# FFN sums of squares: from GpSimd arithmetic to ScalarE squares and accumulating DMAs, in a fused decoder layer

## The reference, cut to what matters

```python
# per batch entry; xf: 512 x 512, h: 512 x 2048
h    = silu(gate(xf)) * up(xf)
inv  = rsqrt(mean(h * h, axis=-1) + eps)          # RMS norm over the 2048 hidden features
y    = (h * inv) @ w_proj.T
x    = layernorm(x + y)
```

## Time and profile before

| | |
|---|---|
| median of 3 runs | 1694.94 us (1691.09 to 1696.45) |
| the profiled execution: its own time | 1689.61 us |
| its span in the trace | 1687.9 us |
| busy: PE, DVE, ACT, POOL | 1235.4, 1269.3, 710.4, 788.3 us |
| FFN squares (L493) and adds (L498) on POOL | 95.0 us in 60 squares (4 more write RD), 121.7 us in 60 adds |
| mean granted TensorE clock | 0.832 of full |

### The profile page before, as it was taken

One profiled execution on the slowest core, in us unless ns is written; L12 is line 12 of the kernel. 1 busy time (PEld: TensorE's weight loads), 2 busy tenths in 40 slices (PEclk: granted clock), 3 DMA queues, 4 the chain that ended last, 5 costly groups with the idle time before them and its releaser, 6 DMA issues.

```text
span 1687.9 us, 13988 instructions
## 1 busy us (share of the span) xinstructions
PE 1235.4 (73%) x4570; PEld 576.9 (34%) x4570; DVE 1269.3 (75%) x1296; ACT 710.4 (42%) x1038; POOL 788.3 (47%) x496
## 2 busy tenths in 40 slices
PE   5564656787887847789786866878797874778696
PEld 4332222333444412333443422323343421323353
DVE  5878879799658876779649885769838887789634
ACT  6773325353354432534363441535354432544221
POOL 1002654244359663334249764334239774334244
PEclk7766878788898977789799986779798886889798
DMA  6742795545136585455236477455235468355132
GB/s 207 261 161 81 163 226 113 129 100 125 53 91 152 114 199 141 101 118 110 67 96 134 111 181 196 88 112 113 69 100 127 112 163 216 89 113 125 36 97 81
DMA packets 108697, 213.88 MB, mean 127 GB/s; under 512 B 13664, under 2 KB 24416, under 8 KB 108624
## 3 DMA queue, kind: packets, MB, share of 16 engines
q1 hardware_dynamic: 89248, 144.95, 30.0%
q0 software_dynamic: 18432, 67.12, 20.8%
q10 hardware_dynamic: 944, 0.92, 0.2%
HBM read 116.08 MB, written 29.62 MB: 86 GB/s over the span
## 4 chain that ended last, share of the span: by engine, by line
DVE 32%; PE 31%; DMA 10%; issue 8%; POOL 6%; ACT 3%; SPq 1%; ACTq 0%; POOLq 0%; DVEq 0%
PE ps L1401 11%; DVE ST L835 11%; DVE MX L891 4%; PE ps L1371 4%; PE ps L1209 4%; DVE ST L838 4%; DMA YA<-ST 4%; DMA GU<-gu_tiles 4%; POOL ST L432 3%; PE ps L1226 3%; DVE QS L1021 2%; DMA KS<-qk_parts 2%; DVE BST L871 2%; PE ps L1315 1%; PE ps L1288 1%
## 5 line engine op out<-in xcount | busy, mean ns | idle before, releaser
L835 DVE TENSOR_TENSOR_SCAN ST<-dA,ST 128x1024 f32<-128x1024 f32 x128 | 383.9, 2999 | 66.8 <-POOL ST L432 49.3
L432 POOL TENSOR_TENSOR ST<-DU,BC 128x1024 f32<-128x1024 f32 x128 | 369.2, 2885 | 134.3 <-issue 61.5
L1401 PE MATMUL ps<-V,GU 128*128 128x512 f16 x1024 | 246.6, 397 | 20.9 <-DMA GU<-gu_tiles 15.2
L446 POOL DMA_DIRECT2D YA<-ST x128 | 112.4, 878 | 301.8 <-DVE ST L838 297.3
L1209 PE MATMUL ps<-KS,QS 96*128 96x512 f32 x256 | 136.1, 607 | 156.4 <-DVE MX L891 73.3
L891 DVE TENSOR_REDUCE MX<-ps 128x1 f32<-128x512 f32 x256 | 165.1, 686 | 111.2 <-PE ps L1209 111.1
L554 ACT ACTIVATE dA<-DL,Aneg 128x511 f32<-128x511 f32 x256 | 167.4, 713 | 142.2 <-DVE ST L835 142.1
L838 DVE TENSOR_TENSOR ST<-ST,BC 128x1024 f32<-128x1024 f32 x128 | 220.8, 1725 | 4.4
L1371 PE MATMUL ps<-WP,QS 128*128 128x512 f32 x512 | 156.1, 453 | 58.3 <-DVE QS L1021 55.2
L685 ACT ACTIVATE PT<-ps 128x1024 f32<-128x1024 f32 x128 | 125.2, 1020 | 138.7 <-PE ps L1315 138.0
L493 POOL TENSOR_TENSOR QAK<-QAK 128x512 f32<-128x512 f32 x60 | 95.0, 1584 | 138.2 <-DVE QAK L1030 138.2
(11 more groups left out here) (220 smaller groups left out, 1704.8 us busy)
## 6 DMA issues: line engine op xcount, KB each, us to landing
YA<-ST POOLq DMA_DIRECT2D x128, 512.0 KB, 5.2
BC<-bc_rows SPq DMA_DIRECT2D x64, 512.0 KB, 5.3
qk_parts<-PT SPq DMA_DIRECT2D x64, 256.0 KB, 5.2
GU<-gu_tiles SPq DMA_DIRECT2D x64, 256.0 KB, 3.6
WP<-proj_tiles SPq DMA_DIRECT2D x64, 256.0 KB, 2.7
QS<-qk_parts SPq DMA_DIRECT2D x48, 256.0 KB, 5.6
KS<-qk_parts SPq DMA_DIRECT2D x48, 256.0 KB, 7.5
ST<-in_L_ffn_w_gate_up_dram SPq DMA_DIRECT2D x16, 256.0 KB, 3.3
```

The costliest lines, as they stand in the source:

```text
L432: nc.gpsimd.tensor_tensor(ST[:, ring(bb, n, a), :, :], DU[:, 2 * a:2 * a + 2, :], BC[:, n % 2, 0:1, :].broadcast_to((P, 2, S)), ALU.mult). ...
L835: nc.vector.tensor_tensor_scan(flat, dA[:, a, :, :].rearrange("p e s -> p (e s)"), flat, 0.0, ALU.mult, ALU.add).then_inc(s_scan, 1)
L1401: last = mm(ps[:, f % F_RING, :], GU[:, t % 2, k, m * P:(m + 1) * P], XHL[:, z, k, :], start=(k == 0 and z == 0), stop=(k == KT - 1 and z ...
```

## The change

POOL's squares and adds go. ACT makes the square of tile t-1 right behind the silu of tile t (tile 15's behind the last HL copy). Square 0 is written into RD. Squares 1 to 15 alternate between two buffers, SQ (even tiles) and a part of PT (odd tiles). POOL adds squares 1 to 14 into RD by accumulating DMAs of 256 KB, each issued when its square is made (`s_sq`) and the accumulation before has landed (`s_acc`, now counted in 16s). ACT writes a buffer again when the DMA that read it has landed. Square 15 isn't accumulated: the final product with ones takes it as a second term, 8 matmuls where there were 4.

```diff
-        SQ = QAK[:, 4, :]
+        SQ = [QAK[:, 4, :], PT[:, 1, 0, :]]
...
+        def squares(t):
+            return RD[:, :] if t == 0 else SQ[t % 2]
+        def sums_landed(b, t):
+            return 16 * (NT - 2) * b + 16 * t
...
                     if not last:
                         for n, a in tile_halves(t):
                             half_step(b + 1, n, a)
-                    pool.wait_ge(s_h, NT * b + t + 1)
-                    if t > 0:
-                        pool.wait_ge(s_acc, NT * b + t)
-                    dst = RD[:, :] if t == 0 else SQ
-                    nc.gpsimd.tensor_tensor(dst, HT[:, t % 2, :], HT[:, t % 2, :], ALU.mult).then_inc(s_sq, 1)
-                    pool.wait_ge(s_sq, NT * b + t + 1)
-                    if t == 0:
-                        pool.sem_inc(s_acc, 1)
-                    else:
-                        nc.gpsimd.tensor_tensor(RD[:, :], RD[:, :], SQ, ALU.add).then_inc(s_acc, 1)
+                    if 0 < t < NT - 1:
+                        pool.wait_ge(s_sq, NT * b + t + 1)
+                        since(pool, s_acc, sums_landed(b, t - 1))
+                        nc.gpsimd.dma_start(RD[:, :], squares(t), accum_op=ALU.add).then_inc(s_acc, 16)
...
+                def square(t):
+                    if t > 2:
+                        act.wait_ge(s_acc, sums_landed(b, t - 2))
+                    nc.scalar.square(squares(t), HT[:, t % 2, :]).then_inc(s_sq, 1)
+
                 for t in range(NT + 1):
                     if t > 0:
                         act.wait_ge(s_h, NT * b + t)
                         if t > 2:
                             act.wait_ge(s_dn, NT * b + t - 2)
                         nc.scalar.copy(HL[:, (t - 1) % 2, :], HT[:, (t - 1) % 2, :]).then_inc(s_hh, 1)
+                        if t == NT:
+                            square(NT - 1)
                     if t < NT:
...
                         nc.scalar.activation(SG[:, t % 2, :], ps[:, (2 * t) % F_RING, :], ACT.Silu).then_inc(s_sg, 1)
+                        if t > 0:
+                            square(t - 1)
...
-                pe.wait_ge(s_acc, NT * (b + 1))
+                pe.wait_ge(s_sq, NT * (b + 1))
+                pe.wait_ge(s_acc, sums_landed(b + 1, 0))
...
                 for r in range(KT):
-                    last = mm(ps[:, 3, r:r + 1], RD[:, r * P:(r + 1) * P], ones[:, 0:1], start=True, stop=True)
+                    mm(ps[:, 3, r:r + 1], RD[:, r * P:(r + 1) * P], ones[:, 0:1], start=True, stop=False)
+                    last = mm(ps[:, 3, r:r + 1], squares(NT - 1)[:, r * P:(r + 1) * P], ones[:, 0:1], start=False, stop=True)
```

## The result

The changed kernel took 1718.06 us (median, 1713.79 to 1723.42) against 1693.01 (1689.70 to 1696.45) for the kernel before, run beside it: ratio 1.0127, 95% interval 1.0094 to 1.0159. The profiled execution took 1713.79 us, its span is 1712.0 at a mean granted clock of 0.830. The forecast was 1677, 1662 to 1697, so the sign was wrong. Of all runs in this document one, an execution of e11 at 1701.27 us, counts as slow (over 1.5% above the fastest of its kernel) and is left out of its ratio.

What follows compares the result with a forecast made beforehand. The prediction took POOL to bound tiles 8 to 16 of three FFN phases. Pairs -9.5, entry -3.0, exit -6.0 and last entry +0.9 gave -17.6 us: 1672 for the profiled execution, 1677 as a median, range 1662 to 1697.

Steps and rivals of the forecast that it cites:

- What bounded the kernel before: Tiles 8 to 16 of three FFN phases: POOL, busy 76.34 of 79 us, with slack in the DMA loop.
- The failed step: Tiles 9 to 15: the pair's tile without a load to wait for hides, so two tiles take 16.5 us.
- the exit: Tiles 15 and 16: the last scan's wait for `dBu` goes; gain of 2.0 us (0 to 3) per entry.
- The nine pairs: Three two-tile intervals, tiles 9 to 15, in each of three entries: 16.5 us for 17.6, -9.5 us in all.
- The road over GU: Tiles 9 to 15: loop product, GU load, gate product, silu, square, `dBu`, scan, product takes 15.95 us before load delay.
- rival 1: Tiles 9 to 15: GU load pays for the whole accumulation, +1.4 for +0.5 us, total 1685 us; chance 0.18.
- rival 2: Tiles 9 to 15: PE's clock falls ahead of the gate product, 1.4 us later; total 1694 to 1703; chance 0.22.
- The rule on the queues' turns: DMA engines alternate between queues packet by packet, so full POOL and SP queues share evenly; 0.5 us allowed for new traffic.
- The entry: Entry to the stage of tiles 8 to 16: first scan's wait and stretching go; gain 1.0 us (0 to 2.5) each.
- The last entry: Last FFN phase: tiles keep PE's pace of 5.33 us, with +0.95 us at the end for the doubled final product.
- rival 3: Last entry: accumulations don't keep PE's pace, about 1.0 us for each of 12 tiles, total 1689 us; chance 0.05.

Runs made afterwards that it cites:

- e11: Changed kernel, but POOL makes the squares instead of ACT, the accumulating transfers staying: 1686.88 us, ratio 0.9929 to the kernel before.
- e3: Changed kernel without the accumulations and their waits, so the squares of tiles 1 to 14 aren't summed: 1683.41 us, ratio 0.9919.
- e7: Kernel before the change, with the GU load issued ahead of the BC row: 1699.51 us, ratio 1.0011.
- e8: Changed kernel with ACT's square of tile t-1 ahead of the silu of tile t: 1709.65 us, ratio 1.0054.
- e15: Changed kernel with POOL's `dBu` held until DVE's product of the half step before is done: 1714.62 us, ratio 1.0102.
- e5: Changed kernel with the GU load issued ahead of the BC row: 1697.33 us, ratio 0.9993; once more 1698.82, 1.0011.
- e10: Changed kernel with square ahead of silu, GU load ahead of BC row, and `dBu` held behind DVE's product: 1652.90 us, ratio 0.9734.
- e2: Changed kernel with each accumulation moving only 32 of 512 columns, all waits and issues kept: 1701.27 us, ratio 1.0047.
- e4: Changed kernel with POOL adding ACT's squares by its own instruction in place of the accumulating DMA: 1703.55 us, ratio 1.0051.
- e6: Changed kernel with each accumulation issued a tile later and moving only 32 of 512 columns: 1703.41 us, ratio 1.0023.
- e9: Changed kernel with both square ahead of silu and GU load ahead of BC row: 1664.60 us, ratio 0.9816.

## Why the prediction was wrong

**What bounded the kernel before** held. POOL set its stage: with part of its work removed e3 and e11 are faster, and e7 shows that the GU road had slack. One reading was loose: POOL's operations run one behind the other, so it is DVE's that stretch them, not each other.

**The failed step** is this one: "The other tile of the pair hides: its gate product follows the down product without a load to wait for, so its square is done about when the scan before it ends." The fact in it was right (square done 540.86, scan end 541.48). The conclusion was not: a `dBu` released at that moment runs beside the product, and the product lasts 2.74 us longer, with the BC row and the GU load of the next odd tile waiting for its end. In the first pair of each entry the `dBu` started 0.5 to 1.0 us behind the product (525.38 behind 524.42 in entry 0) and didn't lengthen it; those are the pairs of 16.6 to 17.1. In the others the product of tile 13 took 3.97, 4.04 and 3.97, and the scan of tile 15 took 5.27, 4.92 and 5.28. The same in "the exit", where I allowed for up to 2.34 into the scan of tile 15 and it was 2.98. The nine pairs were to give -9.5 us (-1.05 each) and gave +19.9. e8 shows that a square that comes earlier only moves the meeting.

This meeting is not the whole price. Taken away alone (e15) it comes back as waits, and the pairs stay at 19.7. With the GU load ahead alone (e5) they are 17.6, as before the change. With both late links mended they are 15.1, and only there is the meeting seen by itself: e10 removes it, 13.6. So the failed step and the road below held each other's loop closed, and how the 2.2 us that a pair grew divide between them no run tells.

**The road over GU** existed as forecast, and four of its terms were too small, in the pair from 13 to 15 of entry 0: product to PE's start 7.11 for 6.0; PE's start to silu 3.46 for 1.94; the scan 5.27 for 2.29; `dBu` with its handoffs 2.81 for 2.44. These are 1.1 + 1.5 + 3.0 + 0.4 = 6.0 (the 3.0 is the same kind of meeting), and 15.95 + 6.0 is the measured 21.9. So the late load of *rival 1* and the clock of *rival 2* came together in the last pair of each entry (gate and up products of 5.31, 6.43 and 4.93 for 3.63, after 2.86, 2.57 and 2.64 us of idle, where I had read "some 3 us" from the earlier trace rows). Rival 2 priced them together at 18.4 to 19.4 for every pair, up to 1703 us, but without the failed step beside them. e2 refutes rival 1's reason, though: with 32 of 512 columns the pairs are the same. The load was as late without any accumulation: the GU loads of tiles 11, 13 and 15 landed in 6.5 to 6.7 us in e3, in 5.6 to 7.2 in the changed kernel, and in 5.2 to 6.1 in the one before. Issued ahead of the BC row (e5) they landed in 2.8 to 5.6. So what makes it late is most likely its place behind the product, together with YA's and BC's transfers; moving it is the only test that was made. The rule on the queues' turns that I cited is not decided by this; that turns by packet mean even shares was my own step.

**The entry** gained 2.4 us an entry, not 1.0 (67.8 to 60.6 in three). But "start", which had no term, lost 1.6 an entry (145.0 to 149.8). The loss is at tile 5: its GU load landed in 6.1 to 6.3 us (5.0 to 5.3 before), and in entry 0 the gate and up products were cold behind it (5.31 us at 466.82). e2, e4 and e6 (145.6 to 146.1) have ACT's extra square and not the bytes, which speaks for the traffic. Two runs don't fit: e3 has no accumulation and 150.7, by a cold 6.31 us at tile 5 of entry 0 alone (its entries 1 and 2 are as before), and e11 has all the bytes and 146.3. So the bytes are the likely cause, not a shown one.

**The exit** gained 0.7 an entry, not 2.0: -2.1 in three. In entry 0 the down product ran cold (3.78 us after 4.27 of idle), and the 16 final products took 3.4 us behind it, at a granted clock of 0.50.

**The last entry** was right: pace 5.33, accumulations landed in 3.3, rival 3 fell; +0.6 for +0.95. The end of the span had no term: +2.5 us.

In sum: -9.5 forecast, +19.9 measured for the pairs; -3.0 and -7.2 + 4.8; -6.0 and -2.1; +0.9 and +0.6; and 8.1 not in the sum. The mechanism that the forecast rested on, POOL relieved, was sound: e3 (which leaves most of the sum out) and e11 gain 0.8% and 0.7%, and with the loops behind it mended the whole change gains 1.8% (e9) and 2.7% (e10), more than the 1.0% that was forecast.

## What to carry to other kernels

Relieving the busy engine can give nothing if its next instruction then stands behind a wait for a longer road: ask what the freed engine's queue waits for (a square behind a silu behind a load behind a product), and cut each link, since cutting one alone gave the pairs a tenth (e8) and a half (e5) of what both gave. Try the halves of a change by themselves: here one half (e11) was a gain and the whole a loss. Where an operation of POOL and one of DVE stretch each other, price the *meeting*, not the durations: an operation that is released earlier may land on the one that everyone waits for, and a deliberate wait there can be a gain (0.8% from e9 to e10), though with the other links left in it gave little or nothing (e15). Loads that no result gates belong ahead of a gated one on the same queue.

## What the runs showed of the hardware

- A DVE product or scan that meets a `dBu` on POOL can last longer by the whole `dBu`: 3.97 - 1.23 = 2.74 beside one of 2.67, 5.27 - 2.29 = 2.98 beside one of 2.98. That is the size of standing still, not of sharing. By the Trainium skill, SBUF — State Buffer, section SBUF: two separate sides, DVE (with two inputs in SBUF) and GpSimd (reading SBUF) share a port pair that is an exclusive lock: whichever starts first has it for its whole instruction, and the other is blocked. The traces agree on the size. Who waits can't be told from the recorded starts when they are close. In both places DVE's row starts ahead, by 0.21 and 0.14 us, and it is DVE that waits. In the attention of the changed kernel a product (at 1383.35, 1.23 us) starts 0.17 ahead of a `dBu`, and there the `dBu` is the longer one (3.26 us for 2.34 with DVE still).
- The last stretch of the span, VE to the end, is 15.7 or 15.8 us in all twelve traces with accumulations into RD by transfers, the thin ones too, and 13.4 in the five without. DVE's work and the four stores there are the same. No row stands in the added 2.5 us. The DMA view shows the four stores, in 40 slices each: e7, 1681 to 1692 us (0.275 us a slice), and e10, 1640 to 1652 us (0.3 us a slice):

```profile
DMA  0000000007970000059800000499089500000000
```
```profile
DMA  0000019910000695000019919930000000000000
```

  In e7 the last packets end in the 32nd slice, about 1689.8, and the span at 1690.6: 0.8 us. In e10 they end in the 27th, about 1648.1, and the span at 1651.2: 3.1 us. What fills the difference was not tried.
